# A decoder layer on one core: the values product in three passes of split operands, the slot buffer cleared in three transfers, and another order at head 13 and at the crossing

## The reference, cut to what matters

```python
# x: (8, 112, 512); ctx: (8, 375, 512)
def attn(x):                                   # 16 heads of 128
    k, q, v = (einsum('ihd,bpd->biph', W, x) for W in (W_K, W_Q, W_V))
    s = einsum('biph,biqh->biqp', k, q); s = causal(s)
    z = einsum('biqp,biph->biqh', softmax(s / sqrt(128)), v)   # the product with the values
    return einsum('df,bqf->bqd', W_O, flat(z))
x = x + attn(layernorm(x))
x = x + cross_attention(layernorm(x), ctx)     # 32 heads of 16, RMS-normed queries and keys
x = x + moe(layernorm(x))                      # 8 experts, top 2, and a shared one
```

## Time and profile before

| | |
|---|---|
| median of 3 runs | 925.3 us (924.29 to 925.62) |
| the profiled execution's own time | 927.61 us |
| its span | 925.8 us |
| busy share | PE 97%, PEld 85%, DVE 65%, ACT 50%, POOL 22% |
| granted TensorE clock, mean | 0.993 of full speed |
| chain that ended last | PE 84%, DVE 8%, ACT 2%, SP's queue 2%, DMA 2% |

### The profile page before, as it was taken

How to read it: one execution, slowest core, us unless ns; L and a number is a source line. 1 busy time by engine, 2 the same in 40 slices (tenths; PEclk the granted TensorE clock), 3 DMA queues, 4 the chain that set the end, 5 groups by cost and what they waited for, 6 DMA issues and landing times.

```text
span 925.8 us, 17938 instructions
## 1 busy us (share of the span) xinstructions
PE 902.5 (97%) x7102; PEld 785.3 (85%) x7102; DVE 597.7 (65%) x1300; ACT 465.7 (50%) x1113; POOL 204.2 (22%) x146
## 2 busy tenths in 40 slices
PE   8999999999999999999999999999999999999995
PEld 8998989799989898777777787777788887999994
DVE  6887575656575635865555655645458857888883
ACT  5533334333334244647666656666574335565651
POOL 0143333223233234301101101011000700223223
PEclk9999999989999999999999999999999999999998
DMA  6221214722212115041101001000032784999973
GB/s 226 59 91 40 94 39 150 232 66 66 90 43 92 40 46 187 23 127 32 59 4 35 25 12 35 12 24 13 3 125 75 266 270 163 349 307 285 302 209 45
DMA packets 40291, 100.94 MB, mean 109 GB/s; under 512 B 7969, under 2 KB 18449, under 8 KB 38289
## 3 DMA queue, kind: packets, MB, share of 16 engines
q1 hardware_dynamic: 35904, 90.62, 29.3%
q0 software_dynamic: 4304, 9.19, 4.9%
HBM read 73.80 MB, written 16.81 MB: 98 GB/s over the span
## 4 chain that ended last, share of the span: by engine, by line
PE 84%; DVE 8%; ACT 2%; SPq 2%; DMA 2%; issue 2%; POOL 0%; DVEq 0%; ACTq 0%
PE bank L562 22%; PE bank L563 21%; PE bank L564 21%; PE bank L816 3%; PE bank L833 3%; PE bank L662 3%; PE bank L638 2%; PE bank L783 1%; DMA wqk_f<-wqk 1%; PE bank L650 1%; PE bank L930 1%; PE bank L843 1%; PE bank L678 1%; SPq L2411 1%; PE bank L938 1%
## 5 line engine op out<-in xcount | busy, mean ns | idle before, releaser
L1310 ACT ACTIVATE ee<-bank 125x448 f32<-125x448 f32 x192 | 91.0, 547 | 22.0 <-PE bank L816 21.0
L1555 DVE TENSOR_TENSOR E_lo<-F,E_hi 128x940 fp32r<-128x940 f32 (+3 forms) x62 | 80.6, 1322 | 3.5 <-ACT E_hi L1080 2.8
L562 PE MATMUL bank<-wkv_hi,ctx_hi 128*125 128x512 f32 x192 | 80.2, 418 | 2.7 <-DVE kn L1829 2.1
L2231 POOL TENSOR_TENSOR ctx_lo<-ctx_f,ctx_hi 128x500 fp32r<-128x500 f32 x24 | 30.4, 1267 | 219.7 <-ACT ctx_hi L1080 219.6
L563 PE MATMUL bank<-wkv_hi,ctx_lo 128*125 128x512 f32 x192 | 76.0, 396 | 0.0
L564 PE MATMUL bank<-wkv_lo,ctx_hi 128*125 128x512 f32 x192 | 75.6, 394 | 0.0
L1838 DVE COPY kT<-bank 128x250 f32<-128x250 f32 x48 | 20.1, 418 | 84.7 <-PE bank L783 84.5
L2231 POOL TENSOR_TENSOR wqk_lo<-wqk_f,wqk_hi 128x1024 fp32r<-128x1024 f32 x14 | 35.1, 2506 | 166.2 <-ACT wqk_hi L1080 166.2
L1080 ACT ACTIVATE E_hi<-F 128x940 fp32r<-128x940 f32 (+3 forms) x62 | 67.6, 1140 | 5.8 <-PE bank L564 4.9
L2340 POOL DMA_INDIRECT out<-yg,meta x21 | 40.0, 1907 | 136.7 <-DVE yg L1979 74.2
L562 PE MATMUL bank<-wv_hi,xT_hi 128*128 128x256 f32 x224 | 64.3, 287 | 0.1
(11 more groups left out here) (391 smaller groups left out, 2599.3 us busy)
## 6 DMA issues: line engine op xcount, KB each, us to landing
F<-wexp SPq DMA_DIRECT2D x14, 1408.0 KB, 7.4
F<-wexp SPq DMA_DIRECT2D x14, 768.0 KB
wqk_f<-wqk SPq DMA_DIRECT2D x16, 512.0 KB, 4.3
ctx_f<-ctx SPq DMA_DIRECT2D x24, 250.0 KB, 2.7
slots<-zt SPq DMA_DIRECT2D x1, 5397.0 KB, 18.7
xg<-slots SPq DMA_DIRECT2D x21, 256.0 KB, 7.2
wv_f<-wv SPq DMA_DIRECT2D x8, 512.0 KB, 5.5
wo_f<-wo SPq DMA_DIRECT2D x8, 512.0 KB, 3.5
```

Of the source, the lines that this page charges most:

```text
L562: e.matmul(out, a[0], b[0], start=first, stop=False)
L1310: e.activation(ee[(4 * n + r) % 8][:, :], SX[r][0:MS, 0:4 * T], ACT.Exp, scale=0.25).then_inc(*x_exped.did((n, r)))
L1555: return e.tensor_tensor(out, src, high.bitcast(F32), ALU.subtract)
L2231: return e.tensor_tensor(out, src, high.bitcast(F32), ALU.subtract)
```

## The change

The probabilities and the values are split, and their product takes three passes. ACT makes every high part, DVE then every low part; both halves of the values' groups and of the turned probabilities go through both engines. `vv` becomes one buffer with high and low parts side by side, so a pair's transfers move twice the bytes, still 14 of them, and wait for the last use of the pair before. They are issued in one lot. The slot buffer is cleared by three transfers, behind the values' of heads 3, 5 and 7. At head 13 the product with the values comes after the scores, and the first unit of head 15's query and key product is put ahead of the output product of pair 6. At the crossing some fillers are exchanged, and `ctx_hi_act(2)` goes to head 14, ahead of the exponentials of head 15. Buffers in SBUF are laid out anew.

```diff
         def behind(h):
             if h == 13:
-                return [("o", 6, j) for j in range(NA)]
+                return qk_uses(NH - 1)[:1] + [("o", 6, j) for j in range(NA)]
...
             def z_pe(h):
                 o = (h % 2) * 128
-                for k in range(2):
-                    w.wait_ge(*v_moved[k][h // 2, len(moves[k]) - 1])
+                w.wait_ge(*v_moved[h // 2, len(moves) - 1])
                 for g in range(2):
                     u = ("z", h, g)
-                    w.wait_ge(*(pt_act if g else pt_dve)[h])
+                    w.wait_ge(*pt_low[h, g])
                     pj_wait(u)
                     for c in range(4):
-                        i = e.matmul(PJ[u][:, c * T:(c + 1) * T], vv[h // 2 % 2][:, 4 * g + c, o:o + 128],
-                                     pt[g][:, c * T:(c + 1) * T], start=True, stop=True)
+                        i = mm3(PJ[u][:, c * T:(c + 1) * T], [vv[:, 4 * g + c, n, o:o + 128] for n in range(2)],
+                                at(pt[g], ALL, toks(c * T, T)), True, True)
...
                 turn_p(h)
+                scores_pe(h + 1)
+                z_pe(h)
                 if h == 13:
-                    z_pe(h)
-                scores_pe(h + 1)
-                if h != 13:
-                    z_pe(h)
-                if h == 13:
+                    qk_pe(NH - 1, *QK[0])
                     o_pe(6, range(NA))
...
             z_pe(NH - 1)
             rows_turn(keys[0])
+            o_pe(last, (0,))
             rows_pe(*keys[3])
-            o_pe(last, (0,))
             rows_turn(keys[1])
...
# ACT
-            def pt_copy(h):
-                w.wait_ge(*p_turned[h, 1])
-                if h:
-                    w.wait_ge(*pj_full["z", h - 1, 1])
-                hi(pt[1][:, :], banks[7][0:T, 0:4 * T]).then_inc(*pt_act.did(h))
+            def pt_hi_act(h):
+                for g in range(2):
+                    w.wait_ge(*p_turned[h, g])
+                    if h:
+                        w.wait_ge(*pj_full["z", h - 1, g])
+                    hi(pt[g][0][:, :], banks[6 + g][0:T, 0:4 * T]).then_inc(*pt_hi.did((h, g)))
...
             tx_hi_act(1)
             tx_hi_act(0)
-            v_act(0, (6,))
+            v_act(0, (4, 6))
...
                     ctx_hi_act(0)
                     qk_act(h + 1, (1,))
                     wkv_hi_act(3)
-                    pt_copy(h)
+                    pt_hi_act(h)
                     ctx_hi_act(1)
+                    ctx_hi_act(2)
                     exp_act(h + 1, (0,))
...
# DVE
-            def v_dve(p, groups):
+            def v_low(p, groups):
                 for b in groups:
-                    u = ("v", p, b)
-                    if p:
-                        w.wait_ge(*v_moved[b // 4][p - 1, len(moves[b // 4]) - 1])
-                    w.wait_ge(*pj_full[u])
-                    e.tensor_copy(vt[:, b:b + 2, :], PJ[u][:, :].rearrange("p (c n) -> p c n", c=2)).then_inc(*pj_dve.did(u))
+                    u, n = ("v", p, b), min(2, NA - b)
+                    w.wait_ge(*v_hi[p, b])
+                    low(vt[:, b:b + n, 1, :], PJ[u][:, 0:256 * n].rearrange("p (c n) -> p c n", c=n), vt[:, b:b + n, 0, :]).then_inc(
+                        *pj_dve.did(u))
...
-            def pt_copy(h):
-                w.wait_ge(*p_turned[h, 0])
-                if h:
-                    w.wait_ge(*pj_full["z", h - 1, 1])
-                e.tensor_copy(pt[0][:, :], banks[6][0:T, 0:4 * T]).then_inc(*pt_dve.did(h))
+            def pt_low_dve(h):
+                for g in range(2):
+                    w.wait_ge(*pt_hi[h, g])
+                    low(pt[g][1][:, :], banks[6 + g][0:T, 0:4 * T], pt[g][0][:, :]).then_inc(*pt_low.did((h, g)))
...
             e.tensor_tensor(t4, b21, t2, ALU.subtract).then_inc(*tx_set.did(0))
-            v_dve(0, (4,))
+            v_low(0, (4, 6))
             tx_low(1)
             shift(0)
...
-                    v_dve((h + 1) // 2, (4,))
-                pt_copy(h)
-                if h == 13:
-                    z_low(h)
+                    v_low((h + 1) // 2, (4, 6))
+                pt_low_dve(h)
                 shift(h + 1)
-                if h != 13:
-                    z_low(h)
+                z_low(h)
                 if h == 0:
                     ws_sum(2)
                 if h == 13:
+                    qk_dve(NH - 1, (0,))
                     o_add(6, range(NA))
                 elif h % 2 == 0 and h < 14:
-                    v_dve(h // 2 + 1, (0,))
+                    v_low(h // 2 + 1, (0, 2))
                 if h == 0:
                     tx_low(2)
...
             rows_finish(*keys[2])
-            wqx_low(1)
-            rows_sum(*keys[3])
             o_add(last, (0,))
             w.wait_ge(*pj_dve["o", last, 0])
             stats(2, 0, T, xa[0:T, 0, :])
-            k_copy(*keys[1])
-            w.wait_ge(*clear[0])
+            wqx_low(1)
+            w.wait_ge(*clear[2])
             w.wait_ge(*padded[0])
             norm_rows(2, 0, T, xa[0:T, 0, :], xn[0])
+            rows_sum(*keys[3])
+            k_copy(*keys[1])
...
# SP
-            def v_move(p, k):
-
-                w.wait_ge(*pj_dve["v", p, 4 * k])
-                w.wait_ge(*pj_act["v", p, 4 * k + 2])
-                if p > 1:
-                    w.wait_ge(*pj_full["z", 2 * p - 3, 1])
-                for i, (b, r, j, z, n) in enumerate(moves[k]):
-                    e.dma_start(vv[p % 2][r:r + n, b, :], vt[z:z + n, j, :]).then_inc(*v_moved[k].did((p, i)))
+            def v_move(p):
+
+                w.wait_ge(*pj_dve["v", p, 6])
+                if p:
+                    w.wait_ge(*pj_full["z", 2 * p - 1, 1])
+                for i, (b, r, j, z, n) in enumerate(moves):
+                    e.dma_start(vv[r:r + n, b, :, :].bitcast(F32), vt[z:z + n, j, :, :].bitcast(F32)).then_inc(*v_moved.did((p, i)))
...
                     wqk_load(h + 2)
-                    v_move((h + 1) // 2, 0)
-                if h == 5:
-                    w.wait_ge(*consts_set["zn"])
-                    e.dma_start(slots_d.rearrange("(u p) d -> p u d", p=128),
-                                zt[:, :].unsqueeze(1).to_broadcast([128, NBLK, RW])).then_inc(*clear.did(0))
-                    e.dma_start(out_d[NT:, :], zt[:, 2:]).then_inc(*padded.did(0))
...
-                        v_move((h + 1) // 2, 1)
+                        v_move((h + 1) // 2)
+                if h in (3, 5, 7):
+                    z = slice((h - 3) // 2 * 7, (h - 3) // 2 * 7 + 7)
+                    w.wait_ge(*consts_set["zn"])
+                    e.dma_start(slots_d.rearrange("(u p) d -> p u d", p=128)[:, z, :],
+                                zt[:, :].unsqueeze(1).to_broadcast([128, 7, RW])).then_inc(*clear.did((h - 3) // 2))
```

More of the change, by code:

```diff
@@ L139, in decoder_layer @@
         mask = sb("mask", [T, T], F32)
-        xn.append(sb("xn1", [128, D], F32))
+        pt_lo0 = over("pt0_lo", [T, 4 * T], F32R, place[0])
+        place[0] += D * 4
         place_f = place[0]
@@ L156, in decoder_layer @@
         place_v = place[0]
-        vv = [sb(f"vv{i}", [T, NB, 256], F32) for i in range(2)]
-        vt = over("vt", [128, NA, 256], F32, place_xs)
+        vv = sb("vv", [T, NB, 2, 256], F32R)
+        vt = over("vt", [128, NA, 2, 256], F32R, place_xs)
         sm = [sb(f"sm{i}", [T, 4, T], F32) for i in range(2)]
         pp = [sb(f"pp{i}", [T, 4, T], F32) for i in range(2)]
-        pt = [sb(f"pt{i}", [T, 4 * T], F32) for i in range(2)]
+        pt_lo = pt_lo0, over("pt1_lo", [T, 4 * T], F32R, place_xs + NA * 2 * 256 * 4)
+        assert NA * 2 * 256 * 4 + 4 * T * 4 <= NB * D * 4
+        pt = [(sb(f"pt{i}_hi", [T, 4 * T], F32R), pt_lo[i]) for i in range(2)]
         place_z = place[0]
@@ L210, in decoder_layer @@
         kn = [sbl(f"kn{i}", [MS, 256], F32, "wv") for i in range(2)]
[L211 removed]
+        vb = [sbl(f"vb{i}", [MS, XH, VW], F32, "wv") for i in range(2)]
         assert room["wv"][0] == place_w + 2 * KC * D * 4 + 2 * XH * 64 * 4
+        vb.append(sbl("vb2", [MS, XH, VW], F32, "wv"))
+        ctx += [pairl(f"ctx{i}", [128, KC, MS], "mid") for i in (2, 3)]
         kT = [sbl(f"kT{i}", [128, 2, MS], F32, "mid") for i in range(6)]
[L214 to L216 removed]
+        assert room["mid"][0] <= place_v
+        room["mid"][0] = place_v
+        vb += [sbl(f"vb{i}", [MS, XH, VW], F32, "mid") for i in range(3, 6)]
         ee = [sbl(f"ee{i}", [MS, 4 * T], F32, "mid" if i < 6 else "z") for i in range(8)]
@@ L437, in decoder_layer @@
         wv_in, wo_in = lane("wv", range(NH // 2)), lane("wo", range(NH // 2))
-        wkv_in, wqx_in, gw_in, clear = lane("wkv", range(KC)), lane("wqx", [0]), lane("gw", [0]), lane("clear", [0])
+        wkv_in, wqx_in, gw_in, clear = lane("wkv", range(KC)), lane("wqx", [0]), lane("gw", [0]), lane("clear", range(3))
         ctx_in = [lane(f"ctx{i}", range(i, NB * MC, 2)) for i in range(2)]
@@ L446, in decoder_layer @@
                 r += row_parts[b][-1][3]
```

(22 more changed lines are left out.)

53 lines of the change are left out of this document (27 added, 26 removed).

## The result

The changed kernel took **946.73 us** (median of 4 runs, 944.33 to 947.96), the kernel before on the same chip 925.46 (4 runs, 924.29 to 927.93): a ratio of 1.0219 [1.0204, 1.0234], some 21 us slower. The direction and the range held; the time lies 7.7 us above the 939.0 that I gave. The profiled execution took 946.11 us, with a span of 944.3 against 925.8, so the two traces differ by 18.5 us.

A forecast was written before the change was run, and what follows sets the result against it. PE was taken to bound the kernel, busy 97% of the span. 14.3 - 6.3 + 4.0 + 1.7 = +13.7 us, added to the median of 925.3, gave 939.0 us, range 930 to 948.

The forecast's parts named there:

- The values product: PE's product with the values: a third weight load adds 0.112 us to each of 128 products, +14.3 us.
- Case A: Rival: in the values product the stream binds, not the load, 0.053 us a pass; 916.4 us, chance 0.10.
- case B: Rival: values product passes of some 0.08 us, +2.2 us in all, 926.9 with the other terms; chance 0.05.
- The clearing: Slot buffer cleared in thirds, with some 20 us to the next needed load: head 6's whole excess goes, -6.3 us.
- The transfers of values: Twice the bytes fit in the gap between heads: nothing, up to 0.5 us at head 0.
- Heads 0 and 1: DVE's list, slowed beside POOL's splits, delays first_sum of head 2: a PE stall of 3.8 us and 0.2, +4.0 us.
- Head 13, 14 and the crossing: Late fourth weight stalls z(14) about 3.1 us; less 0.3 at head 13 and 1.1 at the crossing, +1.7 us.
- D: Rival: the clock falls in both new stalls, 945.6 us; chance 0.25, including the cases of one fall, 942.3.

The follow-up runs named there:

- b_one_at3: The kernel before, with its one clearing transfer of 5.4 MB issued behind the values' transfers of head 3 and the padding's transfer at head 9; 921.47 us.
- a_lots0: The changed kernel, with pair 0's values moved as soon as the groups of two blocks are written, not all behind the last group; 944.83 us.
- a_act14: The changed kernel; on ACT at head 14, projection copy ahead of context's high part, turned probabilities' high part ahead of the fourth cross-attention weight's; 943.0 us.
- a_one_clear: The changed kernel, with all three clearing transfers issued together at the start of head 5, behind the load for head 7; 948.19 us.
- a_unit_back: The changed kernel, with the first unit of head 15's projection again behind the output product of pair 6, on PE and DVE; 944.85 us.
- a_tx_first: The changed kernel, with tx_low(2) and tx_low(3) ahead of the low parts of pair 1's values in DVE's list at head 0; 943.85 us.
- b_clear3_order: b_clear3 (float32 values product kept), with head 13 and the crossing in the change's order on PE, DVE and ACT; 921.79 us.
- a_three: The changed kernel with the edits of a_lots0, a_tx_first and a_act14 together; 940.2 us.
- b_pad_late: The kernel before, with the one clearing transfer in its old place at head 5 and only the output padding's transfer moved to head 9; 923.71 us.
- a_two_pass: The changed kernel with two passes instead of three in the values product, the pass with the low probabilities left out; 933.59 us.
- a_half_low: The changed kernel, with the pass of the low values cut to 64 of its 128 stationary columns; 940.58 us.
- b_clear3: The kernel before, with the clearing in three transfers behind the values' transfers of heads 3, 5 and 7, padding at head 9; 921.56 us.

## Why the prediction was right, and where it was not

**The values product (+14.3): right.** 14.3 us in the trace, and the same 0.89 us a head back with one pass left out. Case A (the stream binds) and case B are refuted by the run with two passes and the one with half of a pass.

**The clearing (-6.3): right in its place, wrong in what it was added to.** Head 6 gave back 6.34 us. But I took the difference of one execution and added it to the median, saying that this was in order. It wasn't: by their mean clock, about half of the executions of the kernel before don't have the fall's 3.3 us. Against the median the term is -3.6. Of my two reasons, thirds instead of one block is wrong (run b_one_at3: the block as a whole does it), and the time until the next load that anything needs is right.

**The transfers of values (0): wrong, two waits of 0.97 and 0.91 us.** SP's queue, changed kernel:

```profile
37.75 8.91 SPq L2374 DMA_DIRECT2D vv<-vt  x14
...
369.17 8.84 SPq L2374 DMA_DIRECT2D vv<-vt  x14
378.05 1.08 SPq L2383 DMA_DIRECT2D ctx_f<-ctx  x2
```

At head 0 they end 0.97 us late, where I had allowed 0.5; run a_lots0 took this wait away. At head 14 I didn't look at what stood behind them. In the kernel before, 6 transfers of 3.73 us stand ahead of the context's load and it is issued at 363.20; here it waits for all 14. ACT waited 4.58 us for that load, with PE's next copy behind it, which is the wait of 0.91 us (gone in run a_act14, where the copy stands first).

**Heads 0 and 1 (+4.0): the mechanism right, the size +6.54.** DVE and POOL there, changed kernel:

```profile
59.86 0.69 DVE L1560 TENSOR_TENSOR vt<-bank,vt 128x512 fp32r<-128x512 f32 x1 [2.00 <-ACT vt L1084]
60.47 2.01 DVE L1560 TENSOR_TENSOR tx2lo<-tx_f2b,tx2hi 128x896 fp32r<-128x896 f32 x1
...
62.60 2.61 DVE L1676 TENSOR_TENSOR pp<-pp,rc 112x448 f32<-112x448 f32 x1
...
66.88 0.61 DVE L1624 TENSOR_TENSOR qk<-part,bank 128x448 f32<-128x448 f32 x1
```

```profile
59.12 2.41 POOL L2232 TENSOR_TENSOR wo_lo<-wo_f,wo_hi 128x1024 fp32r<-128x1024 f32 x1
62.02 2.71 POOL L2232 TENSOR_TENSOR wqk_lo<-wqk_f,wqk_hi 128x1024 fp32r<-128x1024 f32 x1 [0.48 <-ACT wqk_hi L1084]
```

I had `first_sum` end at 66.6 us plus a signal; it ended at 67.49, although the second low part of the values ended at 60.55 and not at 58.4. One normalisation, not two, took 2.6 us beside POOL's split, and `tx_low(2)` 2.01 instead of the 1.08 that `tx_low(3)` took. The trace agrees with what I cited from the Trainium skill (SBUF - State Buffer, Who interferes with whom): `tx_low(2)`, started at 60.47, ended 0.95 us behind POOL's `wo_lo` (59.12 + 2.41). PE was itself 2.7 us late by then (0.97 idle, 1.7 of clock), so its wait was 2.32 and not 3.8. Idling came to 3.1 in all; the other 3.4 are two falls of the clock, of which the point had none. A fall isn't simply added, though: run a_one_clear, without any, lasts only 1.8 us less, in part because PE, not slowed, waits 1.1 us more.

**Head 13, 14 and the crossing (+1.7): +3.9.** The chain to the fourth weight is in the trace as written. ACT, changed kernel:

```profile
381.41 0.62 ACT L1084 ACTIVATE ctx_hi<-ctx_f 128x500 fp32r<-128x500 f32 x1 [4.58 <-DMA ctx_f<-ctx]
...
384.78 1.06 ACT L1084 ACTIVATE wkv_hi<-wv_f 128x1024 fp32r<-128x1024 f32 x1 [2.31 <-DMA wv_f<-wkv]
385.74 0.96 ACT L1084 ACTIVATE pt_hi<-bank 112x448 fp32r<-112x448 f32 x2
```

The stall before z(14) was 2.55 us for 3.1. (I had z(14) start at 371.9 in the kernel before; the trace has 371.61.) The missing terms are 0.91 (above) and 1.7 of clock, and the crossing gave 0.68 where I had 1.1. The wait of 0.57 us that I had given back there is one of 0.67 for DVE's `kT` in the changed kernel.

**Which case.** It was D, 945.6, with a third fall that I hadn't listed. That D's time is within 1.1 us is partly luck: it priced two falls at 3.3 us each, and the trace has three at 1.7. The step that failed is the choice of the point: the one stall of 3 us in the trace had shown the clock falling behind it, and I still forecast two stalls of over 3 us at full clock, because each stood alone in the sum as idle time. Three falls at 1.7 us are 5.1 us, and the idling beside them was close to the 7.1 booked (3.12 + 3.46). With the crossing and head 13 that makes the 4.8 us by which the traces differ more than my sum. Of the other 2.8 to the median, 2.2 is the clearing's term, booked from one long execution, and 0.6 that the changed kernel's profiled execution was shorter than its median. The range held because it took in all of D.

## What to carry to other kernels

A pass with few moving columns costs its weight load: count the stationary columns before adding passes. Price a new stall of PE with the fall of the clock that may follow (here nothing, 1.7 or some 3.3 us), and look in the repeated runs, not only in the profiled one, whether an old stall had it in every execution. Put a large transfer that nobody waits for where the loads behind it aren't needed before it has landed (here some 18 us for 5.4 MB); cutting it up gained nothing here.

## What was not expected of the hardware

The length of the idling did not decide whether the clock fell. It fell behind waits of 0.62 (a_unit_back) and 0.87 us (a_tx_first), and not behind 1.00 (b_clear3_order), 1.49 (a_three), 1.96 (b_pad_late), 2.16 (the wait at 67.91 us in a_act14) or 2.42 us (a_one_clear). The last two runs have the changed kernel's lists at heads 0 and 1, and its own clock fell there, behind a wait of 2.32 us. Windows of run a_act14 around its wait:

```profile
66.00:68.00 2.00, 0.09 (x1) 0.12 (x2) 2.00 (x4) 0.00 (x0) 0.00 (x0) 1.00 0.58 223
68.00:70.00 2.00, 2.00 (x10) 1.87 (x11) 1.79 (x4) 0.00 (x0) 0.00 (x0) 1.00 0.00 0
```

The low stretches lasted 3.4 us in most places and 6.8 in six (before at head 6, a_tx_first at both ends, a_unit_back at head 0, a_two_pass and a_half_low at head 14), which cost 1.7 us or some 3.3. What decides stays open; no run varied it by itself.

The issue behind the 5.4 MB held SP's queue for 7.8 to 8.3 us in three runs (before, b_pad_late, b_one_at3), whatever it was; behind a third of the block it took 0.65 us (b_clear3).
